# Feed-forward weights loaded and summed during the second cross-attention, and its first group normalised at the end of the softmax attention, in a two-layer perceiver kernel

## The reference, cut to what matters

```
x = x + cross_attention_0(layernorm(x), ctx, biases, mask)       # softmax, 16 heads
x = x + polynomial_attention(layernorm(x))
x = x + mixture_of_experts(layernorm(x))                         # 16 experts, top 4, and shared ones
x = x + softmax((layernorm(x) @ ctx.T) / 16 @ ctx)               # second cross-attention
x = x + softmax_attention(layernorm(x), Wqkv) @ Wout + bout      # causal, 16 heads
x = x + feed_forward(layernorm(x), w1, conv_w, conv_b, w2)       # 256 -> 1024 -> 256

def feed_forward(x):                         # both matrices ternary, both inputs in 8 bit
    h = bit_linear(x, w1)                    # 1024 channels
    h = silu(depthwise_conv(h, conv_w, 3 taps along the tokens) + conv_b)
    return bit_linear(h, w2)

def bit_linear(x, w):
    a = 127 / max(max(abs(x), over features), 1e-5);   xq = clip(round(x * a)) / a
    b = 1 / max(mean(abs(w)), 1e-5);                   wq = clip(round(w * b), -1, 1) / b
    return xq @ wq.T
```

## Time and profile before

| | us |
|---|---|
| median of 3 runs | 2396.54 |
| lowest, highest | 2391.7, 2401.5 |
| the profiled execution, its own time | 2406.51 |
| its span (first to last instruction) | 2404.7 |
| in the span: second cross-attention begins | 1577.5 |
| softmax attention's first matmul | 1760.8 |
| feed-forward's block begins | 2049.05 |

### The profile page before, as it was taken

The page is one execution under the profiler, slowest core; times in us unless marked ns, Lnnn a source line. Parts: engine busy times, 40 slices in busy tenths (PEclk is TensorE's granted clock), DMA queues, the critical chain, the costliest instruction groups (busy, mean ns, idle before and its releaser), DMA issues. The chain is left out here.

```text
span 2404.7 us, 57551 instructions
## 1 busy us (share of the span) xinstructions
PE 2142.6 (89%) x19514; PEld 1596.2 (66%) x19527; DVE 1492.1 (62%) x4179; ACT 1099.3 (46%) x2377; POOL 982.8 (41%) x1105
## 2 busy tenths in 40 slices
PE   7999999999899989998999999969978888477773
PEld 5888888888699976565666666646667787233331
DVE  5777777777666663982333333357757776577772
ACT  4666666666544533382222222223335555335442
POOL 3444444444200012444666666521124333036455
PEclk9999999999888989999999999989989999689996
DMA  4110110011000021131222222255500000000002
GB/s 133 32 30 29 38 31 29 29 29 47 2 11 11 9 65 50 44 158 40 85 87 83 87 86 84 78 186 201 199 6 10 7 9 8 35 1 1 0 0 70
DMA packets 120510, 128.80 MB, mean 54 GB/s; under 512 B 77537, under 2 KB 95074, under 8 KB 119138
## 3 DMA queue, kind: packets, MB, share of 16 engines
q1 hardware_dynamic: 105570, 89.23, 12.0%
q0 software_dynamic: 13824, 37.77, 5.0%
q10 hardware_dynamic: 1024, 0.61, 0.1%
HBM read 96.11 MB, written 27.26 MB: 51 GB/s over the span
## 5 line engine op out<-in xcount | busy, mean ns | idle before, releaser
L542 ACT ACTIVATE xa_prob<-xa_neg_s,xa_neg_max 128x256 f32<-128x256 f32 x512 | 224.5, 499 | 143.0 <-DVE xa_neg_max L420 142.9
L1896 PE MATMUL ex_ps_h<-moew_w,ex_xT 128*128 x576 | 274.8, 600 | 4.0 <-issue 1.9
L1944 DVE COPY ex_xT<-ex_ps_x 128x256 f32<-128x256 f32 x144 | 61.2, 425 | 248.2 <-PE ex_ps_x L1903 120.2
L420 DVE CUSTOM_DVE_ANT_0 xa_neg_s<-xa_ps_s,xa_mask 128x256 f32<-128x256 f32 x512 | 191.5, 421 | 33.9 <-PE xa_ps_s L607 19.6
L1873 POOL DMA_INDIRECT ex_xg<-xn_rows,moe_in_row x144 | 140.1, 973 | 111.4 <-issue 62.0
L636 PEld LDWEIGHTS xa_ps_o<-xa_v,xa_probT 128*64 128x64 f32 x4096 | 141.0, 138 | 48.2 <-issue 42.7
L549 ACT ACTIVATE xa_probT<-xa_ps_s 128x512 f32<-128x512 f32 x256 | 152.1, 594 | 41.8 <-PE xa_ps_s L618 40.8
L636 PE MATMUL xa_ps_o<-xa_v,xa_probT 128*64 128x34 f32 x4096 | 169.9, 227 | 0.2 <-ACT xa_probT L549 0.2
L1878 POOL DMA_INDIRECT expert_outs<-ex_y,moe_out_row x144 | 142.6, 990 | 60.0 <-issue 38.4
L1929 ACT ACTIVATE ex_act_g<-ex_ps_h 128x256 f32<-128x256 f32 x144 | 55.3, 384 | 242.9 <-PE ex_ps_h L1896 138.9
L618 PE MATMUL xa_ps_s<-g_ident,xa_prob 128*128 128x128 f32 x1024 | 162.9, 282 | 2.9 <-ACT xa_prob L542 2.7
(11 more groups left out here) (314 smaller groups left out, 5030.1 us busy)
## 6 DMA issues: line engine op xcount, KB each, us to landing
xa_ctxT<-in_ctxT_dram SPq DMA_DIRECT2D x32, 512.0 KB, 3.6
xb_ctx_rows<-in_ctx_rows_dram SPq DMA_DIRECT2D x32, 512.0 KB, 3.7
xb_expert_y<-expert_outs SPq DMA_DIRECT2D x32, 512.0 KB, 4.5
moew_w<-in_moe_w_dram SPq DMA_DIRECT2D x8, 1024.0 KB, 11.8
xn_rows<-rs_xn SPq DMA_DIRECT2D x8, 512.0 KB, 2.9
moew_xw<-in_moe_w_dram SPq DMA_DIRECT2D x8, 512.0 KB, 20.7
out_dram<-g_x SPq DMA_DIRECT2D x1, 4096.0 KB, 13.5
g_x<-in_x_dram SPq DMA_DIRECT2D x2, 1536.0 KB, 15.2
```

What stands on the lines that cost most here:

```text
L420: ins = nc.vector.tensor_tensor_reduce(neg_s[:, u % 2, g, :], ps_s[j][:, g * S:(g + 1) * S], mask[:, b, :], -1.0, 3e38, ALU.add, ALU.min, ...
L542: ins = nc.scalar.activation(prob[:, u % 2, i, :], neg_s[:, u % 2, i, :], ACT.Exp, bias=neg_max[:, u % 2, i:i + 1], scale=-1.0)
L1896: mm = nc.tensor.matmul(ps_h[1 - par][:, :], xT[:, 1 - par, k, :], c.w1[:, own, k, :], start=(k == 0), stop=(k == KC - 1))
```

## The change

The buffers and semaphores that the preparation and group 0 need move into a class `FeedStart`, which is made before the second cross-attention. Its methods are called from three stages.

In the second cross-attention ACT issues the four loads at the block's start, POOL sets the constants behind `following.clear`, ACT sums |w| in steps 3 and 4 (an activation with `Abs` that adds up its outputs, in place of DVE's reduction) and makes the taps in steps 5 to 7, PE adds the sums over the partitions in step 6, and DVE makes mean and inverse in step 7. In the softmax attention DVE takes group 0's statistics behind step 16, POOL forms 1/std behind its last step, and DVE normalises and finds the scales behind step 17. In the feed-forward, DVE begins with the three rounding passes, first all three over w1, then over w2, and group 0 goes straight on to ACT's scaling. PE no longer waits for both matrices at the start: it waits for w1 at its first product and for w2 four groups later.

```diff
+class FeedStart:
+    def load(self, act):
+        act.dma_start(self.w_raw[0][:, :], self.d["ff_w1T"].rearrange("p k n -> p (k n)")).then_inc(self.loaded, 16)
+        act.dma_start(self.w_raw[1][:, :], self.d["ff_w2T"].rearrange("p k n -> p (k n)")).then_inc(self.loaded, 16)
+        act.dma_start(self.cw[:, :, :], self.d["ff_cw"]).then_inc(self.loaded, 16)
+        act.dma_start(self.cb[:, :], self.d["ff_cb"]).then_inc(self.loaded, 16)
+    def set_constants(self, pool, nc):
+        nc.gpsimd.memset(self.rounding[:, 0:1], ROUND).then_inc(self.consts_set, 1)
...
+        nc.gpsimd.memset(self.h[:, :, :, :], 0.0).then_inc(self.consts_set, 1)
+        pool.wait_ge(self.consts_set, 4)
+    def absolute_sum(self, act, nc, i):
+        if i == 0:
+            act.wait_ge(self.loaded, 16 * 4)
+        else:
+            act.wait_ge(self.w_summed, i)
+        nc.scalar.activation(self.tap[:, :, :, :].rearrange("p i j t -> p (i j t)"), self.w_raw[i][:, :], ACT.Abs,
+                             accum_out=self.w_sum[:, i:i + 1]).then_inc(self.w_summed, 1)
+    def taps(self, act, nc, first, last):
+        if first == 0:
+            act.wait_ge(self.w_summed, 2)
+        for j in range(first, last):
+            for i, t in enumerate((0, 2)):
+                ins = nc.scalar.activation(self.tap[:, i, j, :], self.c.ident[:, :], ACT.Copy,
+                                           scale=self.cw[:, j, t:t + 1])
+        ins.then_inc(self.tap_set, last - first)
+    def total(self, pe, nc, ps):
+        pe.wait_ge(self.consts_set, 4)
+        pe.wait_ge(self.w_summed, 2)
+        nc.tensor.matmul(ps[:, E:E + 2], self.ones[:, :], self.w_sum[:, :], start=True, stop=True)\
+            .then_inc(self.w_totalled, 1)
+    def mean(self, dve, nc, ps):
+        dve.wait_ge(self.w_totalled, 1)
+        nc.vector.tensor_scalar(self.w_mean[:, :], ps[:, E:E + 2], 1.0 / (self.F * E), 1e-5, ALU.mult, ALU.max)\
+            .then_inc(self.mean_ready, 1)
+        dve.wait_ge(self.mean_ready, 1)
+        nc.vector.reciprocal(self.w_scale[:, :], self.w_mean[:, :]).then_inc(self.mean_ready, 1)
...
 def cross_attention_1(...)
         def _(pool):
             following.clear(pool, nc)
+            feed.set_constants(pool, nc)
...
                     wait(pe, exp_ready, o - 1)
+                    if isinstance(s, int) and s == 6:
+                        feed.total(pe, nc, ps_o[op])
...
         def _(act):
+            feed.load(act)
+
             def step(s, q):
+                if isinstance(s, int) and s in (3, 4):
+                    feed.absolute_sum(act, nc, s - 3)
+                if isinstance(s, int) and s in (5, 6, 7):
+                    feed.taps(act, nc, 3 * (s - 5), min(3 * (s - 4), feed.FC))
...
         def _(dve):
             def step(s, q):
+                if isinstance(s, int) and s == 7:
+                    dve.wait_ge(o_done, o + 1)
+                    feed.mean(dve, nc, ps_o[o % 2])
                 if live(t):
                     ln.normalise(dve, nc, t, 1 - par, xT_done)
...
 def softmax_attention(...)
             tile_steps(pool, step, n=NP, lag=2)
+            feed.inverse_std(pool, nc, 0)
...
+            def step_and_feed(s, par):
+                step(s, par)
+                if isinstance(s, int) and s == NP:
+                    dve.wait_ge(x_updated, feed.G)
+                    feed.statistics(dve, nc, 0)
+                    feed.aggregates(dve, nc, 0)
+                if isinstance(s, int) and s == NP + 1:
+                    feed.normalise(dve, nc, 0)
+                    feed.scale(dve, nc, 0)
+            tile_steps(dve, step_and_feed, n=NP, lag=3)
...
 def feed_forward(...)
-            dve.wait_ge(loaded, 16 * n_loads)
-            for i in range(2):
-                V.tensor_reduce(w_sum[:, i:i + 1], w_raw[i][:, :], AX.X, ALU.add, apply_absolute_value=True)\
-                    .then_inc(w_summed, 1)
...
+            dve.wait_ge(mean_ready, 2)
             for i, w in enumerate((w1, w2)):
+                ch.then(V.tensor_scalar(w_raw[i][:, :], w_raw[i][:, :], w_scale[:, i:i + 1], ROUND, ALU.mult, ALU.add))
+                ch.then(V.tensor_scalar(w_raw[i][:, :], w_raw[i][:, :], ROUND, 1.0, ALU.subtract, ALU.min))
                 V.tensor_scalar(w[:, :, :].rearrange("p k n -> p (k n)"), w_raw[i][:, :], -1.0, None, ALU.max)\
                     .then_inc(w_ready, 1)
...
-            pe.wait_ge(w_ready, 2)
-            pe.wait_ge(tap_set, 1)
+            pe.wait_ge(tap_set, FC)
```

More of the change, by code:

```diff
@@ L1056, in _, with softmax_attention @@
             tile_steps(pe, step, n=NP, lag=3)
-def softmax_attention(nc, c, X, start):
+def softmax_attention(nc, c, X, start, feed):
     NP = NT // 2
@@ L1963, in cross_attention_1 @@
+def cross_attention_1(nc, c, X, d, following, feed):
     with ExitStack() as ctx:
```

173 lines of the change are left out of this document (86 added, 87 removed).

## The result

The changed kernel took 2372.7 us (median of five runs, 2369.41 to 2378.44) beside 2391.7 us for the kernel before (2388.05 to 2401.5, five runs). The medians differ by 19.0 us. The ratio that was estimated for this comparison is 0.9906, 95% interval 0.9884 to 0.9928, which is 22.5 us of 2391.7 (17 to 28). The 20.2 us that were forecast lie between the two figures. A second measurement gave 0.9913 (0.9898 to 0.9928).

What follows compares the result with a forecast made beforehand. A serial chain of waits between softmax attention and feed-forward, with no group's work on PE, was taken as the bound. -27.4 + 1.0 + 5.2 + 1.0 = -20.2 us from 2396.54 gave 2376.3 us, range 2366 to 2387.

Steps and rivals of the forecast that it cites:

- -27.4 us at the feed-forward: Feed-forward start: the serial preparation ahead of ACT's `ff_xr` goes, since none of it needs softmax attention's last pair; 27.4 us saved.
- just hidden: Feed-forward start: DVE's six chained rounding passes take 7.3 to 7.8 us, within the 7.87 us until `ff_h`.
- +5.2 us at the cross-attention's start: Second cross-attention's start: weight loads delay tile 0 by 5.6 us, less 0.4 us of POOL's old lateness; 5.2 us paid.
- equal bytes: Second cross-attention's start: if both DMA queues get equal bytes, tile 0's loads are complete 2.8 us later.
- packets in turn: Second cross-attention's start: if both DMA queues get equal turns packet by packet, tile 0's loads are 5.6 us later.
- +1.0 us in step 7: Second cross-attention, step 7: DVE waits for PE's product ahead of tile 4's normalisation; 1.0 us lost and not won back.
- +1.0 us in the drain: End of softmax attention: group 0's series on DVE holds up the last pair's reciprocal, so the drain is 1.0 us later.
- ACT hidden: Second cross-attention: ACT's sums and taps are hidden by its waits and cost nothing; without that cover, up to 7 us.
- the start did pay: Against the rival that tile 0's loads are not held up at the cross-attention's start: gain 23.3 us, 2373 us, chance 0.27.
- ACT was not late: Against the rival that late weights delay ACT's copies in the cross-attention, up to 10 us lost: 2381 us, chance 0.13.
- the gain showed: Against the rival that another chain replaces the old one at the feed-forward: gain under 12 us, about 2388 us, chance 0.07.
- the groups' clock stayed at 0.89: Against the rival that PE's granted clock falls in the feed-forward's groups: at 0.77 about 2409 us, chance 0.03.

Runs made afterwards that it cites:

- extra pass: Changed kernel with one rounding pass over w2 done twice, 1.23 us more on DVE; feed-forward block's start to first `ff_h` 8.70 us, no total ratio given.
- weights alone early: Changed kernel with group 0's statistics, root, normalisation and scales back in the feed-forward, only the weights prepared early; 2392.42 us, ratio 0.9969 to the kernel before.
- sums in the tail: Changed kernel with loads and constants later, group 0's root and normalisation a step earlier, weight sums and taps at the cross-attention's end; ratio 0.9906 to the kernel before.
- sums in gaps: As the kernel with the sums in the tail, but ACT's sums and taps moved to where ACT had been idle; ratios 0.9893 and 0.9884 to the kernel before.

## Why the prediction was right

**-27.4 us at the feed-forward:** measured from the blocks' starts 35.35 - 7.87 = 27.5, and 36.67 - 9.33 = 27.3 in column d. The argument (all in series, none of it needs the last pair) held, and so did "just hidden": the passes took 7.54 us against 7.87, within the estimate of 7.3 to 7.8, and the extra pass was paid but for the cover.

**+5.2 us at the cross-attention's start:** tile 0's rows came 4.6 us later (9.48 and 9.32 against 4.86 and 4.78), and its normalisation 4.3 and 4.2 us. The direction and the choice of the upper end were right; the size is 0.9 to 1.0 us too large. The term was made of two figures: 5.6 us of transfers, measured 4.5 to 4.6, at 414 GB/s instead of 375 (2.1 MB are 5.1 us at that rate), and 0.4 us of POOL's old lateness, measured 0.3. By equal bytes the wait would have been 1.05 MB / 414 GB/s = 2.5 us, which the rows exclude; by packets in turn 5.1, which is near. The trace shows the turns and the half microsecond. In the window 1575:1579 the two queues moved (packets, MB, share of the 16 engines)

```profile
q10 hardware_dynamic: 155, 1.14, 67.8%
q1 hardware_dynamic: 154, 0.57, 34.7%
```

where q10 is ACT's queue and q1 SP's: as many packets each, with twice the bytes for the weights. So equal turns are shown. The missing half microsecond is a head start: until 1573.6, 26 packets of the tiles and none of the weights were under way. By my estimate about 256 - 26 = 230 packets of 8 KB then came before tile 0's last, 1.9 MB or 4.6 us at 414 GB/s.

The Trainium skill, in DMA: Bandwidth & Descriptors, section on queues, rings and completion order, has the queues served in turn at the granularity of a packet of 9 to 17 descriptors. The trace agrees with the turns (155 packets against 154 above). It does not show how many descriptors one of its packets holds, and it speaks against turns of whole loads: SP's queue began first, and yet tile 0's first load, `ctx_rows`, landed 5.7 us after its issue, where it took 3.6 before.

**+1.0 us in step 7:** the distance from tile 3's to tile 4's normalisation was 5.83 us in both profiles against 4.86 in both, so 1.0. "It isn't won back" holds: the next distance is 0.3 us shorter (4.82 against 5.09), but the one behind it as much longer (5.52 against 5.25).

**+1.0 us in the drain:** right in kind, smaller in size. In the first profile DVE's reciprocal stood directly behind `ffw_back`, as said, but so did PE's last product:

```profile
2039.70 1.42 PE L1349 MATMUL sa_ps_o<-sa1w_v,sa_w 128*64 128x34 f32 x32
...
2040.99 0.22 DVE L2076 TENSOR_SCALAR ffw_back<-ffw_top,ffw_w_mean 128x4 f32<-128x4 f32 x1
2041.16 0.26 DVE L1157 RECIPROCAL sa_rz<-sa_ps_o 128x16 f32<-128x16 f32 x1
```

It started 1.46 us after that product's start, as in the kernels in which group 0 is not in the way (2042.52 - 2041.06 in the kernel before, 2045.71 - 2044.25 in that with the weights alone early): no delay at all. In the second profile PE was earlier,

```profile
2042.67 1.42 PE L1349 MATMUL sa_ps_o<-sa1w_v,sa_w 128*64 128x34 f32 x32
...
2044.86 0.25 DVE L1157 RECIPROCAL sa_rz<-sa_ps_o 128x16 f32<-128x16 f32 x1
```

and the same distance was 2.19, a delay of 0.73. The term hangs on PE's pace in the last steps (the eight matmuls of L1366 a step earlier took 3.10 us in the first profile and 2.10 in the second); I had named that as its uncertainty.

**ACT hidden:** right for the places the change chose, with half the room I had. The weights' loads ended 13.2 us behind the block's start, where 1588 in the prediction is 10.5, because the two small loads came last; the sum ended 2.7 us before the first Gram copy was wanted, not 5.6. The experiments show how thin that is: with the sum at 19.1 us instead of 13.2 behind the block's start ACT is the late one. The second sum cost nothing that can be seen: from tile 2's to tile 3's normalisation are 6.82 and 6.87 us with it, and 6.81 in the kernel with the sums in the tail, which has no sum there.

**Sum.** The stages c and d of the two pairs of profiles give 5.8 - 27.4 = -21.6 and 6.2 - 27.3 = -21.1, and with 0 and 0.7 for the drain -21.6 and -20.4, against the predicted -20.2. Between medians -19.0 and -21.0 were measured, by the ratios -22.5 and -20.9. That the sum came so close is in part luck, for two errors cancel. The start cost 0.9 to 1.0 us less than forecast, and the drain up to 1.0 less; but between tile 1's and tile 3's normalisations 0.5 and 1.0 us more went by than in the kernel before, for which the prediction had no term. That loss is not one of the places that the change chose: the kernel with the sums in the tail has 0.7 to 0.9 us of it, and the two profiles of the kernel with the sums in gaps differ there by 1.1 us, with the same instructions and with PE's first matmuls faster in the one that is shorter. The forecast of 2376.3 us for the median was 3.6 us above; the step that is off by most is the unchanged one, the base of 2396.54 us: the kernel before had a median of 2391.7 in that measurement, 4.8 us lower. Of the rivals none came: the start did pay, ACT was not late, the gain showed, and the groups' clock stayed at 0.89.

## What to carry to other kernels

A preparation that stands alone between two stages is worth its whole length, but only when everything in series there moves: here the weights' part alone gave 13 us and left 14. Its new place costs by queue: a load beside the first tile's rows, a memset ahead of the first 1/std, a sum ahead of an exponential each cost 1 to 5 us, and removing the largest only uncovered the next. A wait for four loads lasts as long as the smallest of them if that is issued last (2.8 us here). So find each engine's idle stretch by the timeline and put the piece behind the instruction that ends there. Where effects are 1 to 5 us and runs spread by 5, compare stages from their own start in two profiles of each kernel, not totals.

## What the runs showed of the hardware

A DVE normalisation of 128x256 from one SBUF operand took 2.12 us instead of 0.41 beside a POOL memset of 1.86 us (two kernels), while in the kernels whose memset waited for that normalisation DVE's four additions with two SBUF inputs took their usual 2.04 us beside the same memset, and the normalisation 0.41. In the kernel with the sums in gaps the two stood so:

```profile
1597.87 1.86 POOL L2009 MEMSET ffw_h<- 128x2112 f32 x1
...
1598.10 2.04 DVE L2213 SCALAR_TENSOR_TENSOR g_x<-xb_expert_y,moe_weight,g_x 128x256 f32<-128x256 f32 x4
```

The Trainium skill, in SBUF — State Buffer, section "Who interferes with whom", says that DVE's `tensor_scalar` can enter a mode that takes the port pair shared with GpSimd, the other engine then fully blocking, and that an instruction with two SBUF inputs contends only with a GpSimd one that reads. The additions agree (2.04 us beside a memset, which reads nothing). The normalisation agrees in that it ended 0.14 us behind the memset in both kernels (1602.74 and 1602.60 us in the one shown); that it was in such a mode, no row shows. In the changed kernel the memset met an addition, which took its 2.04 us, and not a normalisation.

The distance from tile 0's normalisation to the first Gram copy was 4.06 and 4.30 us in two profiles of the kernel before, 4.30 and 4.61 in two of the kernel with the sums in gaps. The first fence is from the kernel before, the second from the second profile of the kernel with the sums in gaps: the same 16 matmuls of the first tile, after a pause of 19.7 us.

```profile
1587.46 4.80 PE L2026 MATMUL xb_ps_g<-xb_ctx_rows 128*128 128x256 f32 x16
```

```profile
1575.95 6.11 PE L2151 MATMUL xb_ps_g<-xb_ctx_rows 128*128 128x256 f32 x16
...
1582.11 3.62 PE L2151 MATMUL xb_ps_g<-xb_ctx_rows 128*128 128x256 f32 x16
```

The next 16 took 3.62 us. The windows of that second kernel (columns as in the earlier trace rows) give the clock:

```profile
1570.00:1580.00 10.00, 4.53 (x12) 3.73 (x13) 6.41 (x16) 0.40 (x1) 5.35 (x9) 0.50 0.80 322
1580.00:1590.00 10.00, 10.00 (x50) 8.04 (x50) 5.92 (x17) 4.44 (x8) 0.79 (x2) 0.95 0.69 269
```

It is at its lower level (1.2 GHz) until about 1580 and near its upper one behind that: the clock rises while PE is busy with the first tiles, and where in it differs from run to run. In the first profile of the same kernel these 16 matmuls took 5.04 us instead of 6.11, a microsecond that column c inherits.
